# The scan of a two-layer fp32 kernel: where in a step the high and low half of a feed-forward tile are made

## The reference, cut to what matters

```
# test-time-training attention: 32 chunks of 16 tokens, one after the other
def step(carry, x):                      # W1_s is 16x16 per head and batch
    Z1 = xk @ W1_s + b1_s
    grad = _ln_fused_l2_bwd(Z1, xv - xk, ln_w, ln_b)
    ...
    W1_new = W1_s - (last_eta * xk).swapaxes(-1, -2) @ grad
# feed-forward, 2048 tokens, 512 -> 1408 -> 512, ternary weights
g = einsum('th,ih->ti', xf, gate_w) * gate_s
u = einsum('th,ih->ti', xf, up_w) * up_s
hdn = silu(g) * u
out = einsum('ti,hi->th', hdn, down_w) * down_s
```

## Time and profile before

| | |
|---|---|
| median of 3 runs | 2056.87 us (2054.27 to 2058.54) |
| the profiled execution | 2057.76 us, of which the span from first to last instruction is 2055.8 us |
| mean granted TensorE clock in it | 0.976 of full speed |
| the scan in it | from about 195 to about 870 us of the span |
| steps 0 to 8 / 9 to 31 | about 198 to 352 us / 352 to 760 us |

### The profile page before, as it was taken

The page is one execution under the profiler, slowest core; times in us unless marked ns, Lnnn a source line. Parts: engine busy times, 40 slices in busy tenths (PEclk is TensorE's granted clock), DMA queues, the critical chain, the costliest instruction groups (busy, mean ns, idle before and its releaser), DMA issues. The chain is left out here.

```text
span 2055.8 us, 34803 instructions
## 1 busy us (share of the span) xinstructions
PE 1897.7 (92%) x12632; PEld 1432.0 (70%) x12632; DVE 1199.4 (58%) x2368; ACT 1003.7 (49%) x2169; POOL 1026.5 (50%) x904
## 2 busy tenths in 40 slices
PE   5897998898998999798899989999999999999998
PEld 3676776666666665487677766777777777777776
DVE  4662565686876764355334446666666666666653
ACT  3332555565565655466433325444444444444442
POOL 5453566566655654420133317655555555555552
PEclk9998999999999999989999999999999999999999
DMA  7776647335434432131578772122233223322321
GB/s 247 281 284 211 202 152 267 106 116 208 119 114 155 164 110 97 52 125 67 200 239 258 240 264 82 60 113 92 83 131 117 87 84 131 115 83 83 113 96 48
DMA packets 157111, 297.97 MB, mean 145 GB/s; under 512 B 20240, under 2 KB 97296, under 8 KB 150288
## 3 DMA queue, kind: packets, MB, share of 16 engines
q1 hardware_dynamic: 155856, 294.70, 42.4%
q10 hardware_dynamic: 1088, 1.05, 0.2%
HBM read 221.52 MB, written 74.19 MB: 144 GB/s over the span
## 5 line engine op out<-in xcount | busy, mean ns | idle before, releaser
L1975 POOL TENSOR_SCALAR probs<-probs,rsum 128x512 f32<-128x512 f32 x256 | 396.1, 1565 | 245.6 <-DVE rsum L2111 245.6
L2075 ACT ACTIVATE p_tok<-bank 128x512 fp32r<-128x512 f32 x256 | 154.5, 607 | 344.1 <-PE bank L2015 344.0
L2107 DVE TENSOR_REDUCE nmax<-bank 128x1 f32<-128x512 f32 x256 | 158.9, 682 | 95.5 <-PE bank L2007 95.5
L2117 DVE TENSOR_TENSOR p_tok<-bank,p_tok 128x512 fp32r<-128x512 f32 x256 | 173.2, 679 | 15.8 <-ACT p_tok L2075 15.8
L2067 ACT ACTIVATE probs<-bank,nmax 128x512 f32<-128x512 f32 x256 | 172.8, 692 | 3.6 <-DVE nmax L2107 3.6
L1456 POOL TENSOR_TENSOR y_pieces<-y_tok,y_pieces 128x512 fp32r<-128x512 f32 x48 | 61.4, 1296 | 210.3 <-ACT y_pieces L1670 210.3
L60 PE MATMUL bank<-xs,ffn_w 128*128 128x512 f32 x352 | 152.6, 434 | 12.2 <-issue 8.4
L2015 PE MATMUL bank<-ident,probs 128*128 128x128 f32 x1024 | 155.7, 276 | 2.8 <-DVE p_tok L2117 2.8
L2015 PEld LDWEIGHTS bank<-ident,probs 128*128 128x128 f32 x1024 | 121.5, 140 | 50.8 <-issue 27.2
L1090 DVE SCALAR_TENSOR_TENSOR pt<-bank,t_mask 128x256 f32<-128x256 f32 x256 | 91.7, 413 | 98.0 <-PE bank L877 96.7
L61 PE MATMUL bank<-xs,ffn_w 128*128 128x512 f32 x352 | 138.7, 394 | 0.0
(11 more groups left out here) (279 smaller groups left out, 4980.0 us busy)
## 6 DMA issues: line engine op xcount, KB each, us to landing
ffn_w<-ffn_pieces SPq DMA_DIRECT2D x120, 512.0 KB, 3.6
uvo<-uvo_pieces SPq DMA_DIRECT2D x15, 2048.0 KB, 8.4
wq<-wq_pieces SPq DMA_DIRECT2D x16, 1536.0 KB, 6.3
ffn_pieces<-stage SPq DMA_DIRECT2D x30, 512.0 KB, 4.1
xs<-xn_pieces SPq DMA_DIRECT2D x4, 2048.0 KB, 8.1
y_tok<-in_gup SPq DMA_DIRECT2D x32, 256.0 KB, 3.1
wk<-wk_pieces SPq DMA_DIRECT2D x16, 512.0 KB, 3.6
ffn_w<-ffn_pieces SPq DMA_DIRECT2D x16, 384.0 KB, 3.5
```

What stands on the lines that cost most here:

```text
L1975: nc.gpsimd.tensor_scalar(probs[:, u % 8, :], probs[:, u % 8, :], rsum[:, u % 8:u % 8 + 1], None, ALU.mult).then_inc(norm_done, 1)
L2075: nc.scalar.activation(p_tok[:, Q % 2, 0, :, hh * P:(hh + 1) * P], banks[4 + u % 2][:].rearrange("p (k q) -> p k q", k=NBLK), ACT.Copy).th ...
L2107: nc.vector.tensor_reduce(nmax[:, u % 8:u % 8 + 1], banks[u % HG][:], axis=X_AXIS, op=ALU.max, negate=True).then_inc(max_done, 1)
L2117: nc.vector.tensor_tensor(p_tok[:, Q % 2, 1, :, q], banks[4 + u % 2][:].rearrange("p (k q) -> p k q", k=NBLK), p_tok[:, Q % 2, 0, :, q].bi ...
```

## The change

For every segment the changed kernel works out `in_front(n, i, j)`: the ups that ended in this segment before a down j that follows a gate or an up; and `ups_left(n, i)`: the ups that ended in the segment and stand in front of no such down. On ACT and on POOL the high and the low half of the first sort are made in front of that down; those of the second in a new `settle(n, i)` behind the segment. No instruction is added or taken away: 44 highs and 88 halves of low stand elsewhere in the order.

- ACT: `settle(n, 0)` stands behind segment 0, the second `spread_q` and the `spread_grad`, and in front of the wait for `sg_done`; `settle(n, 1)` behind `expand`, `turned_k` and the output copies, in front of `spread_grad`; `settle(n, 2)` right behind segment 2, so in front of the next step's warm and its wait for z; `settle(n-1, 3)` in front of segment 0 of step n.
- POOL: each settle right behind its segment; `settle(n, 0)` is so in front of `sum_s`, `settle(n, 1)` in front of `snapshot_w`.

```diff
+            ups_in = lambda js: [j for j in js if kind_of(j) == "up"]
+            in_front = lambda n, i, j: ups_in(ended(n, i)[:ended(n, i).index(j)]) if kind_of(j) == "down" and kind_of(j - 1) != "down" else []
+            ups_left = lambda n, i: [u for u in ups_in(ended(n, i)) if not any(u in in_front(n, i, j) for j in ended(n, i))]
...
 # POOL
                     def ffn(n, i):
                         for j in ended(n, i):
-                            if j >= 1 and kind_of(j - 1) == "up" and kind_of(j) != "down":
-                                low(nth(j - 1))
                             if kind_of(j) == "up":
                                 product(nth(j))
-                                if kind_of(j + 1) == "down":
-                                    low(nth(j))
+                            for u in in_front(n, i, j):
+                                low(nth(u))
                             if kind_of(j) == "down":
                                 add_down(j)
+
+                    def settle(n, i):
+                        for j in ups_left(n, i):
+                            low(nth(j))
...
                     for n in range(END):
+                        if n >= 1:
+                            settle(n - 1, 3)
                         ffn(n, 0)
+                        settle(n, 0)
                         if n < NSTEP:
                             sum_s(n)
...
                         ffn(n, 1)
+                        settle(n, 1)
...
                         ffn(n, 2)
+                        settle(n, 2)
...
 # ACT
-                            if j >= 1 and kind_of(j - 1) == "up" and kind != "down":
-                                high(j - 1)
+                            for u in in_front(n, i, j):
+                                high(u)
                             act.wait_ge(f_ready, j + 1)
...
-                                if kind_of(j + 1) == "down":
-                                    high(j)
...
+                    def settle(n, i):
+                        for j in ups_left(n, i):
+                            high(j)
...
                         if ps:
                             spread_q(ps[0])
+                        if n >= 1:
+                            settle(n - 1, 3)
                         ffn(n, 0)
                         if ps:
                             spread_q(ps[1])
                             spread_grad(ps[0])
+                        settle(n, 0)
                         if n < NSTEP:
                             act.wait_ge(sg_done, n + 1)
...
                             nc.scalar.activation(o_sq[:], obank[:], ACT.Square).then_inc(osq_done, 1)
+                        settle(n, 1)
                         if ps:
                             spread_grad(ps[1])
                         ffn(n, 2)
+                        settle(n, 2)
                     late(END - 1)
+                    settle(END - 1, 3)
```

## The result

The changed kernel takes **2081.73 us** (median of 4 runs, 2080.02 to 2082.32) against 2057.7 (4 runs of the kernel before, 2054.27 to 2060.06): ratio 1.0119, interval 1.0104 to 1.0134. It is slower by 24 us. The forecast was 2061.4 with a range up to 2065.0: the direction was right, the size was wrong by a factor of five, and the result lies outside the range.

The account below looks back on a forecast made before the run. TensorE, busy 92% of the span, was taken as the bound, so only its idle time could change. Terms of +4.85, -0.4 and 0 gave +4.5 us on 2056.87: 2061.4, range 2056.5 to 2065.0.

Parts of the forecast that it names:

- Step 8: Early phase: ACT's high waits for its product in front of the square, so PE's job starts later: +2.45 us.
- Step 1: Early phase: late product and high delay the square by 2.6 us, the chain gets somewhat shorter: +1.9 us.
- no wait there hangs on a moved instruction: 0: Steps 32 to 43: they have no chain and no wait depends on a moved instruction, so 0 us.
- steps 10 to 31 at -0.4: Middle steps: three patterns of gains (-3.1) and losses (+2.7) in segment 0 and highs before squares, together about -0.4 us.
- in step 13 it is set off ... : 0: Segment 2's high before the next square: its remaining delay is offset by a low-half wait that goes, 0 us.
- the 0.6 for step 29: Step 29: DVE's sg_bd copies slow beside a low half; 0.6 us, also covering what segment 2's high leaves before the square.
- Rival 1: The clock falls in step 8, perhaps step 1, losing some 1.6 us each time: 2063 to 2065; chance 0.15.
- Copies beside a low: Chain-bound steps: one pair of DVE copies takes between 0.77 and 1.60 us, giving -2 to +3 around the sum.
- the change of table: ACT's table change costs 1.3 us without a drain; with the skill's drain the sum would be about 1.6 larger.
- the second (stalls covered): Rival: ACT's new stalls before squares in steps 1, 2 and 8 are covered: 2056 to 2060; chance 0.26.
- the third (faster): Rival: waits for low halves and gates' evictions come back while losses are 2 us: 2051; chance 0.09.
- The fourth: Rival: the order that matters is unchanged, so the longest low-half wait, 4.3 us, stays; no chance of its own.

Follow-up runs that it names:

- e4: Changed kernel, but from step 10 on POOL makes segment 0's low half behind sum_s, spread_k and snapshots, those of segments 1 and 2 behind the output work: 2062.10 us.
- e1_early: Kernel before the change, with new places only for the ups that end in steps 0 to 9: 2064.37 us, ratio 1.0031.
- e10_best: Kernel before, with POOL's order of e4 and new places only for up 7 and, from step 10 on, all but ups 16, 18, 33, 35: 2050.31 us.
- e8: Changed kernel, but from step 10 on POOL makes only segment 0's low half behind sum_s, spread_k and the snapshots: 2079.04 us, ratio 1.0105.
- e7_segments12: Kernel before the change, with new places only for ups that end in segments 1 and 2: 2070.54 us, ratio 1.0056.
- e5_gainers: Kernel before the change, with new places only for ups 7, 17, 23, 26 and 34: 2056.50 us, ratio 0.9998.
- e6_segment0: Kernel before the change, with new places only for ups that end in segment 0: 2058.17 us, ratio 1.0008.

## Why the prediction was wrong

**The early phase: the mechanism was right.** Step 8 was forecast at +2.45 and measured at +2.43, by the steps written down. The timeline of the kernel after answers to the earlier trace rows:

```profile
339.12 1.43 POOL L740 TENSOR_TENSOR hid<-up_sb,silu_g 128x256 f32<-128x256 f32 x2
...
340.58 0.63 ACT L995 ACTIVATE hid_hi<-hid 128x512 fp32r<-128x512 f32 x1 [2.98 <-POOL hid L740]
341.23 1.28 ACT L1036 ACT_TABLE_LOAD   x1
...
342.64 0.37 ACT L1038 ACTIVATE t<-bank 128x256 f32<-128x256 f32 x1
...
345.11 0.69 ACT L1007 ACTIVATE silu_g<-bank,ffn_scales 128x512 f32<-128x512 f32 x1
...
345.89 0.47 PE L60 MATMUL bank<-xs,ffn_w 128*128 128x512 f32 x1 [3.35 <-issue]
```

High waits 2.98 for the product, load and warm stand behind it, the square comes at 342.64, and PE's gate job finds its bank not evicted for 3.35. Steps 3 and 4 came to +1.21 and -1.80 for +1.3 and -1.5. Step 1's square was forecast at about 223.5 and came at 223.33, but the step grew by 0.83, not 1.9, and step 2 by 1.27, not 0.5: together 2.1 for 2.4. Steps 6 and 9 were +0.69 and +1.75 for -0.3 and +0.5; their idle times changed by -0.16 and +0.25, and the rest is the clock. The whole phase: +6.1 for +4.85. The prediction's terms are idle time, and of that there is 3.7; the sum comes nearer to 6.1 than its terms deserve, because steps 1 and 2 had been put too high (2.4 for 1.7) and the clock, put at nothing, added 2.5.

**The term that failed first: "no wait there hangs on a moved instruction: 0", for steps 32 to 43.** It measured +9.1 (the window's +8.2 holds step 31, which is 0.9 shorter), 6.7 of it idle time. The waits for `q_bd` hang on POOL's queue: two of the four in the kernel before grew from 0.9 to 2.6, and two new ones came. The orders around the change were known: `settle(n, 1)` and `settle(n, 2)` pass the output work on POOL, and the scores' wait for `q_bd`, 0.86 in each of four steps, was in the list of waits. The price could have been taken from rows: a low of 1.43 and its wait for high, against an `o_std` that started only 0.46 after POOL was ready for it. The prediction looked at which waits the change takes away there and found none; it did not ask what stands behind the moved low on POOL. `e4` shows it: with the low half behind the output work, idle time in steps 32 to 42 is 0.6 us below that of the kernel before.

**The second: steps 10 to 31 at -0.4.** They measured +8.5 (9.3 up to step 30, -0.9 in step 31), 4.1 of it idle time. The single patterns were well read: step 12 -0.98 for -0.75, step 28 -0.99 for -0.65, step 27 +0.97 for +0.9, step 11 +0.38 for +0.4, step 17 +0.57 for +0.6, step 18 -0.42 for -0.2, step 21 -0.68 for -0.2, step 31 -0.87 for -0.4. In step 12 ACT's `sg_bd` starts 0.50 behind the end of `sg`, as foretold. What failed is "in step 13 it is set off ... : 0", measured +3.11, and the 0.6 for step 29, measured +2.48. Both were worked out by adding settles that each stood alone. The product of the second up was taken to follow its eviction as in the kernel before. But the first up's high was moved behind the gate's Silu, as the prediction itself says of step 12, and it did not ask what waits for that high: POOL's low half, in an order that the change leaves as it was, and behind it `sum_s`, `spread_k` and that product. That 44 lows change place on POOL, as the section on the change has it, or all save six, as the prediction has it, is not so: by the orders of the two programs 23 of the 44 lows stand where they stood among POOL's other work. Where an up and its next gate end in the same segment, as in segment 0 of steps 12, 15, 18, 19, 21, 28 and 31, only the high moves, and to a later place. Steps 15 and 19 were counted as gains of 0.45; they lost 2.14 and 0.87 (0.52 and 0.86 of idle time). There the low of the step before passes `w_snap_x` and `o_std`, and they lose nothing in `e4`, so it was POOL's order.

**The third: the clock.** Rival 1 gave it 1.6 us a time, at one or two places, with a chance of 0.15. The price was right: 1.60 in step 8 of `e1_early`. The places were not: in the changed kernel it did not fall in step 8, but it fell in steps 9, 13, 15, 16, 35 and 39 where it had not before, and stayed down longer in step 6. That is 9.2 of the 24 us; it is already inside the +6.1, +8.5 and +9.1 above. It was named as a sign of being wrong ("the clock lower at places that I don't name"), but it belongs to the sum, not to a rival: where a change adds stalls at ten places, falls come with them in this kernel, though not always in the step that has the stall (step 16 has no added idle time). What sets the place of a fall stays open.

**Two bounds that held.** Copies beside a low were put between 0.77 and 1.60. In step 29 of the kernel after they take 1.58, at the upper end, and `sum_s`, which stood beside them before, is now behind:

```profile
734.73 1.47 POOL L747 TENSOR_TENSOR hid_lo<-hid,hid_hi 128x256 fp32r<-128x256 f32 x2 [0.74 <-ACT hid_hi L995]
...
734.76 1.58 DVE L1147 COPY sg_bd<-sg 32x256 f32<-32x256 f32 x2
```

In step 17 they take 1.45 and in both steps of the kernel before 0.77. The other is the change of table: in the rows above the warm-up and square follow the load at once, with no drain between them. The Trainium skill ("ScalarE: Activation LUTs", "What ACT_TABLE_LOAD costs") states one of about 1.38; this trace does not agree with it, and the sum was right to leave it out.

Of the rivals, the second (stalls covered) and the third (faster) are wrong as cases of this kernel. But a gain exists once the moves that lose are taken out: 6.1 us of idle time in `e10_best`. It does not come where the third rival had it. In that kernel's waits over the scan,

```profile
PE bank L877 <- DVE sg_bd L1170: 11.2, 13, 1.9
...
PE bank L60 <- issue: 6.7, 8, 1.5
```

the chain's are 6.0 shorter than in the earlier trace rows, of which 2.0 stand under another releaser, and those for a bank 1.7; the waits for a low half are no shorter in sum, as step 16 gives back what step 4 gained. An eviction and an `sg_bd` that ACT starts earlier are what pays.

The fourth (the longest wait for a low half, in step 6, stays) held: it is 4.7 long now, for 4.3.

## What to carry to other kernels

When an instruction is moved forward in an in-order queue, price everything that it passes on each queue, with its own wait for its input added to its length, and also in stretches where the move gains nothing: here POOL's low half in front of the output work was the larger part of the loss (9.3 of the 14.5 us of idle time lie between `e8` and `e4`). When one is moved backward, do the same for what waits for it on the other queues: a high 1.9 us later made `sum_s` and a product late on POOL. Cost several such moves together, as one delays the input of the next. And choose them one by one by what the trace shows that each gains: as a rule for all this move cost 1.2%, as a choice, with POOL's order mended, it gave 0.4%.

## What was not expected of the hardware

- Equal idle time does not give an equal clock. Step 8 has idle time of 3.35 us in three kernels (after, `e4_pool_order`, `e8_low_behind_sum`) with a granted clock of 1.00, and of 3.36 in `e1_early` and `e7_segments12` with 0.91. The length and idle time of the step don't tell the two apart. But nothing was saved: in the three kernels that kept the clock in step 8 it fell in step 9 instead (0.91), and steps 8 and 9 together have about 1.5 us more busy time than before in all five. What sets the place stays open. For the time it means that gains and losses in idle time of a few us carry an uncertainty of one or two falls, some 1.6 us each: it took back nearly all of `e5_gainers` (idle -3.8 us, time 0.9998), and `e6_segment0`, whose idle time fell by 0.5, has runs from 2055.7 to 2064.3.
- How much a copy on DVE is slowed beside POOL's work differs with the kind of that work. A pair takes 0.77 beside `sum_s` and 1.58 beside a two-input subtraction. The Trainium skill ("SBUF — State Buffer", "SBUF: two separate sides") describes the port pair that DVE and POOL share as a lock of which the loser is blocked in full; the copies that end with the low half agree with that, those beside `sum_s` do not show such a block.
